# Attention and MoE block on one core: a head pair in four stages of eight score units instead of eight stages of four, and all 32 pairs written out

## The chip, the cores and the metric

One Trainium2 core (core 0) runs the whole kernel; the other seven are idle. The metric is the device time of one execution in microseconds (us), median of three runs. Each engine executes its own instruction list in order and waits for others by semaphores: PE (TensorE, matmuls), ACT (ScalarE), DVE (VectorE), POOL (GpSimd) and SP (here only a queue that issues DMAs).

## The reference

The input is 4 sequences of 1024 tokens with 128 channels, in float32. Attention has 16 heads of 64 channels, the mixture of experts has 8 experts with room for 512 tokens each. Cut to what matters:

```python
h = layernorm(x)
q, k, v = (einsum('bsd,hdk->bhsk', h, w) for w in (w_q, w_k, w_v))
weights = softmax(einsum('bhqk,bhmk->bhqm', q, k) / 8, axis=-1)
z = einsum('bhqm,bhmk->bhqk', weights, v)
x = x + h + concat_heads(z) @ w_o
h2 = layernorm(x)
probs = softmax(h2 @ Wr); expert = argmax(probs); rank = tokens of that expert before this one
y[token] = prob * (relu(h2[token] @ W1[expert]) @ W2[expert])   if rank < 512
x = x + h2 + y
```

## The kernel before, in words

**Pairs.** Two heads of one sequence are handled together, a *pair*; there are 32 pairs, 8 for each sequence, and they take most of the time. A pair works on score tiles of 128 keys by 512 queries. For each half `h` of the 1024 queries there are 8 key tiles `kt` and 2 heads `p`, so 16 *units* for a half and 32 for a pair. A unit is two matmuls on PE (`scores`, L957 and L958: high parts, then corrections and the maximum) into a PSUM bank `ps_s`, and one exponential on ACT (`unit`, L557) from that bank into the SBUF tile `ring`. POOL adds up the exponentials of each key tile for the softmax sums (`add_up`, L425), and PE multiplies them by the values into `ps_z` (`values`, L969).

**Maxima.** Before a half can start, the maximum of each query's scores must be known. PE computes plain scores for 128 queries and all keys of both heads (`max_scores`, L935, a *visit*, four matmuls into the two double banks `ps_m`), DVE reduces them (`reduce_max`, L762, twice per visit), PE turns the result (`turn_max`, L947), ACT copies it (`copy_max`, L542, tile `mxt`) and SP places it with two small DMAs. There are 8 visits per pair, made for the halves that come next.

**The next pair's operands.** Meanwhile the next pair's queries and keys are projected (`project_qk`, L914 to L916, in four uses of three matmuls), ACT casts each to its high part (`cast_qk`, L523), DVE subtracts to get the low part (`low_qk`, L757) and SP places the parts with six DMAs. `project_v` (L923) and `copy_v` (L537) make the values, `project_out` (L987) and `add_wo` (L780) the output product.

**After the values.** `softmax_sums` (L979) adds up over keys with ones on PE, DVE takes reciprocals in four quarters (`recip`, L768) and scales (`scale_z`, L775).

**The order** is written by hand. A pair has 8 *quads*: in each, PE does 4 units, with one or two projections between the second and the third, then one visit and the values of two key tiles. `ps_s` has two banks, so a unit waits for the exponential of the unit two before it. Pairs 0 and 1 and pairs 24 to 31 are written out, pairs 2 to 23 run in a loop of two pairs on every engine (`LOOP_FROM`, `UNROLL_FROM`). Pairs 0 and 1 also hold the layer norms and turns of the later sequences, and the DMAs that clear the slots in HBM (`clear_slots`, issued by ACT, all four after pair 1). In the last 8 pairs the first three sequences are routed (`routed`, roles a, b, c): moments, norm, logits, ranks, and `scatter`, eight indirect DMAs on POOL (L404), all eight in a row. The tokens' high and low parts (`h_high`, `h_low`) are made anew for every pair on ACT and POOL (L531, L411) from a copy `hTs` that a DMA brings.

**Then** the last sequence is routed, and the experts run one after the other.

## Time and profile before

| | us |
|---|---|
| median of 3 runs (lowest to highest) | 1688.39 (1686.33 to 1690.32) |
| the profiled execution, its time | 1693.12 |
| its span, first to last instruction | 1691.4 |
| PE busy | 1557.2 (92% of the span) |
| POOL busy | 1249.9 (74%) |
| DVE busy | 1071.8 (63%) |
| ACT busy | 790.6 (47%) |

The profiled execution is 4.7 us above the median, and its own time is 1.7 us above its span. Busy time of PE is modelled: the rows of two matmuls that follow each other overlap, so their starts tell more than their durations.

### The profile page before, as it was taken

How to read it: one execution, taken by the hardware profiler on the slowest of the kernel's cores; microseconds unless marked ns; L12 is line 12 of the kernel's file. 1: busy time of each engine (PE TensorE's matmuls, PEld its weight loads, DVE VectorE, ACT ScalarE, POOL GpSimd, SP SyncE). 2: the span in 40 equal slices, each digit the busy share in tenths (PEclk: the TensorE clock that was granted, in tenths of full speed). 3: DMA queues.
4: the chain of work that ended last, by engine and by line, in shares of the span. 5: the costliest groups of instructions: out<-in, count | busy, mean ns of one | idle time of the engine just before them, and what ended most of it. 6: DMA issues, size and time to landing. Idle time of an engine off the chain costs nothing.

```text
span 1691.4 us, 24966 instructions
## 1 busy us (share of the span) xinstructions
PE 1557.2 (92%) x7396; PEld 851.1 (50%) x7396; DVE 1071.8 (63%) x1316; ACT 790.6 (47%) x1543; POOL 1249.9 (74%) x713
## 2 busy tenths in 40 slices
PE   2898999999999999999999999999998989989286
PEld 1354555555555555555555555555454545544165
DVE  4565666666666767666667676666675676753332
ACT  1454555455545554545454545454554545534221
POOL 2586887777788888787888777778878778777225
PEclk8799999999999999999999999999998999989588
DMA  5333333333333333333333333333321343210430
GB/s 137 92 92 134 86 83 82 93 93 93 93 93 93 93 92 91 80 86 79 79 73 83 83 93 93 93 93 94 92 76 52 88 119 92 52 52 13 155 118 35
DMA packets 118578, 148.71 MB, mean 88 GB/s; under 512 B 41482, under 2 KB 62479, under 8 KB 118016
## 3 DMA queue, kind: packets, MB, share of 16 engines
q1 hardware_dynamic: 115392, 137.73, 32.1%
q0 software_dynamic: 2560, 6.14, 1.0%
q10 hardware_dynamic: 576, 4.23, 0.6%
q8 instruction: 26, 0.43, 0.1%
q14 instruction: 24, 0.20, 0.0%
HBM read 18.91 MB, written 12.65 MB: 19 GB/s over the span
## 4 chain that ended last, share of the span: by engine, by line
PE 82%; POOL 5%; DVE 5%; issue 3%; ACT 2%; DMA 1%; SPq 1%; another core or an unknown queue 0%; ACTq 0%; POOLq 0%; DVEq 0%
PE ps_z L969 26%; PE ps_s L957 16%; PE ps_s L958 13%; PE ps_m L935 10%; PE ps_x L979 3%; PE ps_x L987 3%; POOL acc L425 2%; DVE mxw L762 2%; PE ps_m L923 2%; PE ps_x L923 1%; POOL tokens_by_slot L404 1%; PE ps_x L914 1%; PE ps_x L915 1%; PE ps_x L916 1%; PE ps_z L1186 1%
## 5 line engine op out<-in xcount | busy, mean ns | idle before, releaser
L425 POOL TENSOR_TENSOR acc<-acc,ring 128x1024 f32<-128x1024 f32 x382 | 909.6, 2381 | 186.3 <-ACT ring L557 165.5
L557 ACT ACTIVATE ring<-ps_s 128x512 f32<-128x512 f32 x1024 | 555.9, 595 | 586.2 <-PE ps_s L958 508.0
L762 DVE TENSOR_REDUCE mxw<-ps_m 128x1 f32<-128x1024 f32 x512 | 602.9, 1219 | 234.8 <-PE ps_m L935 229.2
L969 PE MATMUL ps_z<-ring,V 128*64 128x512 f32 x2048 | 497.8, 607 | 0.0
L957 PE MATMUL ps_s<-queriesA,keysA 128*128 128x512 f32 x1024 | 450.1, 440 | 11.6 <-ACT ring L557 10.3
L958 PE MATMUL ps_s<-queriesB,keysB 65*128 65x512 f32 x1024 | 409.3, 400 | 0.0
L957 PEld LDWEIGHTS ps_s<-queriesA,keysA 128*128 128x128 f32 x1024 | 195.3, 191 | 230.8 <-issue 181.2
L768 DVE RECIPROCAL ps_x<-ps_x 128x128 f32<-128x128 f32 x256 | 221.9, 925 | 65.8 <-PE ps_x L979 65.8
L425 POOL TENSOR_TENSOR acc<-ring 128x1024 f32<-128x1024 f32 x64 | 151.2, 2363 | 135.3 <-ACT ring L557 135.3
L969 PEld LDWEIGHTS ps_z<-ring,V 128*64 128x64 f32 x2048 | 124.7, 136 | 241.5 <-issue 171.6
L935 PE MATMUL ps_m<-keysA,queriesA 64*128 64x512 f32 x1024 | 190.6, 450 | 26.3 <-DMA queriesB<-qk_rest 13.4
L958 PEld LDWEIGHTS ps_s<-queriesB,keysB 65*128 65x128 f32 x1024 | 196.6, 192 | 29.0 <-issue 1.0
L935 PEld LDWEIGHTS ps_m<-keysA,queriesA 64*128 64x128 f32 x1024 | 77.6, 187 | 150.3 <-issue 123.0
L757 DVE TENSOR_TENSOR qk_rest<-ps_x,qk_high 128x512 fp32r<-128x512 f32 x94 | 65.1, 692 | 133.0 <-ACT qk_high L523 132.9
L548 ACT ACTIVATE zr<-ps_z 128x512 f32<-128x512 f32 x64 | 38.2, 597 | 118.6 <-PE ps_z L969 114.4
L979 PE MATMUL ps_x<-acc,ones 128*64 128x512 f32 x256 | 70.0, 619 | 25.3 <-POOL acc L425 25.3
L780 DVE TENSOR_TENSOR x<-ps_x,x 128x512 f32 (+1 forms) x63 | 43.1, 685 | 53.8 <-PE ps_x L987 53.8
L411 POOL TENSOR_TENSOR h_low<-hTs,h_high 128x1024 fp32r<-128x1024 f32 x30 | 71.8, 2392 | 0.0
L987 PEld LDWEIGHTS ps_x<-wo,zT 128*128 128x128 f32 x504 | 63.7, 192 | 7.4 <-issue 0.5
L987 PE MATMUL ps_x<-wo,zT 128*128 128x128 f32 x504 | 66.4, 275 | 0.0
L460 POOL DMA_INDIRECT out<-ye,ring x32 | 31.1, 973 | 47.3 <-DVE ye L862 39.3
L523 ACT ACTIVATE qk_high<-ps_x 128x512 fp32r<-128x512 f32 x94 | 56.1, 597 | 11.3 <-PE ps_x L911 4.2
(143 smaller groups left out, 1015.7 us busy)
## 6 DMA issues: line engine op xcount, KB each, us to landing
queriesA<-qk_high SPq DMA_DIRECT2D x256, 128.0 KB, 2.4
keysA<-qk_high SPq DMA_DIRECT2D x128, 128.0 KB, 2.3
keysB<-qk_high SPq DMA_DIRECT2D x128, 128.0 KB, 2.3
keysA<-qk_rest SPq DMA_DIRECT2D x128, 128.0 KB, 2.3
queriesB<-qk_rest SPq DMA_DIRECT2D x128, 128.0 KB, 2.3
hTs<-hT SPq DMA_DIRECT2D x30, 512.0 KB, 3.3
tokens_by_slot<-rows ACTq DMA_DIRECT2D x4, 1032.0 KB, 8.7
ring<-tokens_by_slot SPq DMA_DIRECT2D x8, 516.0 KB, 7.4
```

Of the source, the lines that this page charges most:

```text
L411: pool.tensor_tensor(h_low[:, :], hTs[par][:, :], h_high[:, :].bitcast(F32), ALU.subtract).then_inc(low_split, 1)
L425: pool.tensor_tensor(acc[h][:, :], before, P_both(kt), ALU.add).then_inc(summed, 1)
L557: act.activation(P_tile(kt, p), ps_s[u % 2][:, :], ACT.Exp, scale=SCALE).then_inc(exp_done, 1)
L757: dve.tensor_tensor(qk_rest[s][:, :], qk_bank(j, use), qk_high[s][:, :].bitcast(F32), ALU.subtract).then_inc(qk_low, 1)
L762: dve.tensor_reduce(mxw[h][:, p * HT + qt:p * HT + qt + 1], ps_m[p][:, :], AX_X, ALU.max).then_inc(maxed, 1)
L768: dve.reciprocal(ps_x[:, c], ps_x[:, c]).then_inc(recip_done, 1)
L935: mm = pe.matmul(ps_m[p][:, kh * HALF:(kh + 1) * HALF], queriesA[par][p][r, at:at + P], keysA[par][p][r, kh * HALF:(kh + 1) * HALF], start ...
L957: pe.matmul(ps_s[p][:, :], keysA[par][p][:, k], queriesA[par][p][:, c], start=True, stop=False)
L958: pe.matmul(ps_s[p][:, :], keysB[par][p][:, k], queriesB[par][p][:, c], start=False, stop=True).then_inc(scores_ready, 1)
L969: mm = pe.matmul(ps_z[p * DK:(p + 1) * DK, :], V[par][:, kt * P + p * DK:kt * P + (p + 1) * DK], P_tile(kt, p), start=(kt == 0), stop=(kt ...
L979: mm = pe.matmul(ps_x[p * DK:(p + 1) * DK, :], ones[:, :], part, start=(i == 0), stop=(i == len(parts) - 1))
L987: mm = pe.matmul(bank[:, i * P:(i + 1) * P], zT[h][:, i * P:(i + 1) * P], wo[par][:, :], start=True, stop=True)
```

## The change

A pair now has 4 *octs* instead of 8 quads. In an oct PE does three units, `project_qk`, two units, then `project_v` or `project_out` (and, in every second oct, `turn_max`), three units, a visit, the values of four key tiles, in octs 0 and 2 the softmax sums, and a second visit. The counts of matmuls stay. What else changes:

- `ps_s` gets a third bank. The bank `ps_x` is gone: projections, turns and products now borrow halves of `ps_m` (`lent_qk`, `lent_turn`, `lent_out`, `lent_max`) between visits, and the softmax sums use `ps_s[2]`. So a projection waits until DVE has reduced the visit before it, and a visit waits until ACT and DVE have read what was lent.
- The sums are first copied by ACT to an SBUF tile `sums` (`copy_sums_out`, new), and `recip` and `scale_z` read that tile instead of PSUM.
- For the last of the four uses ACT writes the key's high part itself (`key_direct`), and its DMA is dropped.
- The tokens' high and low parts are made once for each sequence (at pairs 0, 6, 14 and 22) instead of once for each pair; `hTs` and its DMA are gone. `w_high` and `w_low` have two buffers.
- The slots are cleared from a small tile `blank`, one DMA at the end of each oct of pair 1. `rows` has two buffers, routing is spread over roles a to e, and a sequence's eight scatters go one at a time between the additions, six in one pair and two in the next.
- The moments of sequences 2 and 3 are taken on DVE before pair 0, and their roots on POOL.
- `LOOPED` is empty: every engine has all 32 pairs written out.

The diff, cut to its core:

```diff
-        ps_s = [ctx.enter_context(nc.psum_tensor(f"ps_s{i}", [P, HALF], F32)) for i in range(2)]
+        ps_s = [ctx.enter_context(nc.psum_tensor(f"ps_s{i}", [P, HALF], F32)) for i in range(3)]
...
+        lent_qk, lent_turn = ps_m[1][:, 0:HALF], ps_m[1][:, HALF:S]
+        lent_out, lent_max = ps_m[0][:, 0:HALF], ps_m[0][:, HALF:S]
...
+        LOOPED = []
...
+            def copy_sums_out(j, h):
+                act.wait_ge(sums_done, 2 * j + h + 1)
+                act.wait_ge(z_ready, 2 * j + h)
+                act.activation(sums[:, :], ps_s[2][:, :], ACT.Copy).then_inc(sums_copied, 1)
...
+                    for k in range(3):
+                        unit(j, oct, k)
+                    if oct < 2 and not last:
+                        cast_qk(j + 1, nxt, 2 + oct)
+                    if oct >= 2 and not known(j, LAST - 1, LAST):
+                        cast_qk(j + 2, par, oct - 2)
+                    unit(j, oct, 3)
+                    if oct in (0, 2) and not last:
+                        copy_v(j + 1, nxt, oct // 2, lent_out)
+                    unit(j, oct, 4)
...
+                if not (known(j, 0) and oct == 0 and k < 3):
+                    if k == 0:
+                        pe.wait_ge(exp_done, 2 * UNITS * j + 8 * oct)
+                    if k >= 3:
+                        pe.wait_ge(exp_done, 2 * UNITS * j + 8 * oct + k - 2)
...
-                dve.tensor_tensor(zT[h][:, :], ps_x[:, :], zr[h][:, :], ALU.mult).then_inc(z_ready, 1)
+                by = ps_s[2] if known(j, LAST) and h == 1 else sums
+                dve.tensor_tensor(zT[h][:, :], by[:, :], zr[h][:, :], ALU.mult).then_inc(z_ready, 1)
...
+                        if routed(j, "d") is not None and kt in (3, 5, 7):
+                            scatter(routed(j, "d"), [3 * h + kt // 2 - 1])
+                        if routed(j, "e") is not None and h == 0 and kt in (3, 5):
+                            scatter(routed(j, "e"), [6 + kt // 2 - 1])
...
+                    if visits:
+                        visit(v, 0)
+                    values(j, par, oct)
+                    if oct == 0 and not first:
+                        softmax_sums(j - 1, 1)
+                    if oct == 2:
+                        softmax_sums(j, 0)
+                    if visits:
+                        visit(v + 1, 1)
```

How PE's list changes in the middle of a pair. Before, after two units of a quad come the rest of that quad: a projection (L914 to L916), two units (L957, L958), a visit (L935) and the values of two key tiles (L969):

```order
L914 MATMUL ps_x<-h_high,w_low 128x512
L915 MATMUL ps_x<-h_low,w_high 128x512
L916 MATMUL ps_x<-h_high,w_high 128x512
L957 MATMUL ps_s<-queriesA,keysA 128x512
L958 MATMUL ps_s<-queriesB,keysB 128x512
L957 MATMUL ps_s<-queriesA,keysA 128x512
L958 MATMUL ps_s<-queriesB,keysB 128x512
L935 MATMUL ps_m<-keysA,queriesA 128x512 x4
L969 MATMUL ps_z<-ring,V 64x512 x4
```

Now, at the end of oct 2 of pair 0, after five units: three units (L1004, L1005), a visit (L970), the values of four key tiles (L1018), the sums (L1028) and the second visit:

```order
L1004 MATMUL ps_s<-queriesA,keysA 128x512
L1005 MATMUL ps_s<-queriesB,keysB 128x512
L1004 MATMUL ps_s<-queriesA,keysA 128x512
L1005 MATMUL ps_s<-queriesB,keysB 128x512
L1004 MATMUL ps_s<-queriesA,keysA 128x512
L1005 MATMUL ps_s<-queriesB,keysB 128x512
L970 MATMUL ps_m<-keysA,queriesA 128x512 x4
L1018 MATMUL ps_z<-ring,V 64x512 x8
L1028 MATMUL ps_s<-acc,ones 64x512 x2
L970 MATMUL ps_m<-keysA,queriesA 128x512 x4
```

Units now stand eight together where four stood, and the values eight where four did.

On ACT the copy of the values' projection (`V`) stood between two pairs of exponentials of a quad, in a written-out pair of before:

```order
L557 ACTIVATE ring<-ps_s 128x512 x2
L537 ACTIVATE V<-ps_x 128x512
L557 ACTIVATE ring<-ps_s 128x512 x2
L533 ACTIVATE w_high<-wst 128x256
```

Now it stands ahead of the fifth exponential of an oct, here in an even oct of pair 2:

```order
L569 ACTIVATE zr<-ps_z 128x512
L583 ACTIVATE ring<-ps_s 128x512 x3
L542 ACTIVATE qk_high<-ps_m 128x512
L583 ACTIVATE ring<-ps_s 128x512
L558 ACTIVATE V<-ps_m 128x512
L583 ACTIVATE ring<-ps_s 128x512 x4
```

The third unit after the copy is the eighth of the oct, which on PE waits for the fifth exponential.

On DVE, quads 1 to 3 of a written-out pair of before (reciprocals L768 from PSUM, low part L757, scaling L775, maxima L762, output added L780):

```order
L768 RECIPROCAL ps_x<-ps_x 128x128 x2
L757 TENSOR_TENSOR qk_rest<-ps_m,qk_high 128x512
L768 RECIPROCAL ps_x<-ps_x 128x128 x2
L775 TENSOR_TENSOR zT<-ps_x,zr 128x512
L762 TENSOR_REDUCE mxw<-ps_m 128x1 x2
L757 TENSOR_TENSOR qk_rest<-ps_x,qk_high 128x512
L762 TENSOR_REDUCE mxw<-ps_m 128x1 x2
L780 TENSOR_TENSOR x<-ps_x,x 128x512
```

Now, from the scaling of an even oct to the second visit of the odd oct that follows (the four reductions in a row are the first visit of one oct's end, and the second visit's, reduced in the next oct):

```order
L800 TENSOR_TENSOR zT<-sums,zr 128x512
L778 TENSOR_TENSOR qk_rest<-ps_m,qk_high 128x512
L783 TENSOR_REDUCE mxw<-ps_m 128x1 x4
L792 RECIPROCAL sums<-sums 128x128
L778 TENSOR_TENSOR qk_rest<-ps_m,qk_high 128x512
L792 RECIPROCAL sums<-sums 128x128
L805 TENSOR_TENSOR x<-ps_m,x 128x512
L783 TENSOR_REDUCE mxw<-ps_m 128x1 x2
L792 RECIPROCAL sums<-sums 128x128 x2
```

Two reciprocals, the low part and the output's addition now stand between the reductions of the last visit and those of the next one, and the scaling has both inputs in SBUF.

## Rows read from the trace of the kernel before

**Rows 1.** Busy time by stretch: PE, PEld, DVE, ACT, POOL; clock, DMA share, GB/s

```profile
600.00:700.00 100.00, 100.00 (x478) 53.80 (x475) 68.08 (x71) 50.03 (x99) 82.17 (x38) 1.00 0.31 79
```

**Rows 2.** Timeline of ACT: copies of turned maxima, one per half pair; start, duration

```profile
74.93 0.25 ACT L542 ACTIVATE mxt<-ps_m 8x128 fp32r<-8x128 f32 x1
...
150.15 0.25 ACT L542 ACTIVATE mxt<-ps_m 8x128 fp32r<-8x128 f32 x1
...
180.14 0.25 ACT L542 ACTIVATE mxt<-ps_m 8x128 fp32r<-8x128 f32 x1
...
609.33 0.25 ACT L542 ACTIVATE mxt<-ps_m 8x128 fp32r<-8x128 f32 x1
...
631.47 0.25 ACT L542 ACTIVATE mxt<-ps_m 8x128 fp32r<-8x128 f32 x1
...
654.46 0.25 ACT L542 ACTIVATE mxt<-ps_m 8x128 fp32r<-8x128 f32 x1
...
1150.92 0.25 ACT L542 ACTIVATE mxt<-ps_m 8x128 fp32r<-8x128 f32 x1
...
1173.22 0.25 ACT L542 ACTIVATE mxt<-ps_m 8x128 fp32r<-8x128 f32 x1
...
1540.05 0.25 ACT L542 ACTIVATE mxt<-ps_m 8x128 fp32r<-8x128 f32 x1
```

**Rows 3.** Timeline of PE in the loop, pieces of three quads

```profile
604.72 0.40 PE L958 MATMUL ps_s<-queriesB,keysB 65*128 65x512 f32 x1
605.05 0.73 PE L935 MATMUL ps_m<-keysA,queriesA 64*128 64x512 f32 x4
605.71 1.94 PE L969 MATMUL ps_z<-ring,V 128*64 128x512 f32 x8
607.58 0.50 PE L957 MATMUL ps_s<-queriesA,keysA 128*128 128x512 f32 x1
607.92 0.39 PE L958 MATMUL ps_s<-queriesB,keysB 65*128 65x512 f32 x1
608.15 0.39 PE L957 MATMUL ps_s<-queriesA,keysA 128*128 128x512 f32 x1
...
616.40 1.94 PE L969 MATMUL ps_z<-ring,V 128*64 128x512 f32 x8
618.16 1.03 PE L979 MATMUL ps_x<-acc,ones 128*64 128x512 f32 x4
```

**Rows 4.** Timeline of PE and of ACT around a `project_v` of a written-out pair

```profile
1490.15 1.05 PE L923 MATMUL ps_x<-wst,hTs 128*128 128x128 f32 x8
...
1491.24 0.60 ACT L537 ACTIVATE V<-ps_x 128x512 f32<-128x512 f32 x1 [0.20 <-issue]
1491.77 1.09 ACT L557 ACTIVATE ring<-ps_s 128x512 f32<-128x512 f32 x2
```

**Rows 5.** Timeline of DVE in the loop

```profile
605.82 2.35 DVE L762 TENSOR_REDUCE mxw<-ps_m 128x1 f32<-128x1024 f32 x2 [0.69 <-PE ps_m L935]
...
619.24 1.78 DVE L768 RECIPROCAL ps_x<-ps_x 128x128 f32<-128x128 f32 x2 [0.38 <-PE ps_x L979]
621.71 0.69 DVE L757 TENSOR_TENSOR qk_rest<-ps_m,qk_high 128x512 fp32r<-128x512 f32 x1 [0.69 <-ACT qk_high L523]
```

**Rows 6.** Timeline around a DVE instruction with both inputs in SBUF

```profile
1269.98 2.37 POOL L425 TENSOR_TENSOR acc<-acc,ring 128x1024 f32<-128x1024 f32 x1
...
1271.34 1.10 DVE L741 TENSOR_TENSOR logits<-one_hot,logits 128x64 f32<-128x64 f32 x1
```

**Rows 7.** Timeline of POOL and PE at a scatter: one of eight, and PE afterwards

```profile
1276.20 0.98 POOL L404 DMA_INDIRECT tokens_by_slot<-rows,scatter_at  x1 [0.30 <-issue]
...
1289.83 1.98 PE L979 MATMUL ps_x<-acc,ones 128*64 128x512 f32 x4 [7.82 <-POOL acc L425]
```

**Rows 8.** Timeline of ACT after the four clearing DMAs

```profile
160.42 1.08 ACT L557 ACTIVATE ring<-ps_s 128x512 f32<-128x512 f32 x2 [8.38 <-issue]
```

**Rows 9.** Groups by line, all of the run: xcount, busy us, mean ns, idle before

```profile
L665 DVE BATCH_NORM_STATS2 moment_parts<-x 128x6 f32<-128x128 f32 x64 | 13.8, 277 | 3.5 <-DMA x<-in_L_attn_x 3.3
```

More of the change, by code:

```diff
@@ L559, in pair @@
-            def pair(j, par, first=False, last=False, early=None, route=False, split=True, next_first=True):
+                act.wait_ge(scores_ready, 2 * UNITS * j + 8 * oct + k + 1)
+                act.activation(P_tile(kt, p), ps_s[k % 3][:, :], ACT.Exp, scale=SCALE).then_inc(exp_done, 1)
+            def pair(j, par, b):
                 nxt = 1 - par
-                a, turns = (routed(j, "a"), routed(j, "b")) if route else (None, None)
-                for quad in range(QUADS):
-                    h, u = quad // 4, 4 * (quad % 4)
-                    if not first and quad == 1:
+                last = known(j, LAST)
+                for oct in range(OCTS):
+                    if oct == 0 and not known(j, 0):
@@ L829, in _ @@
+                    if routed(j, "c") is not None and oct == 3:
+                        find_slots(routed(j, "c"), 1)
             for use in range(4):
                 low_qk(0, use)
-            for v in range(5):
+            for v in range(4):
                 for p in (1, 0):
                     reduce_max(v, v // 4, v % 4, p)
-            low_qk(1, 0)
-            pair(0, 0, first=True, early=0)
-            pair(1, 1, early=1)
-            with dve.Fori(0, LOOPS) as i:
-                for par in range(2):
-                    pair(2 * i + LOOP_FROM + par, par)
@@ L1079, in pair @@
[L1079 to L1092 removed]
+                    if c is not None and oct < 2:
+                        turn_h2(c, oct)
@@ new lines, in pair @@
+                    if c is not None and oct == 2:
+                        make_logits(c)
+                    if c is not None and oct == 3:
+                        count_ranks(c)
+                    if oct == 1:
+                        turn_max(j, 1, lent_max)
+                    if not last and oct == 3:
+                        turn_max(j + 1, 0, lent_max)
+                    for k in range(5, 8):
+                        scores(j, par, oct, k)
+                    v = 8 * j + 6 + 2 * oct
```

731 lines of the change are left out of this document (351 added, 380 removed).

## The prediction

> **What bounds the kernel now.** I read three views: the busy time by stretch, ACT's timeline for the rhythm of the pairs, and PE's timeline for what a pair consists of. In the loop PE is busy 100.00 of 100 us, DVE 68, POOL 82, ACT 50, at full clock [rows 1]: PE bounds it, and there is nothing to win by shortening a wait. The copies of the maxima mark half pairs: 609.33 to 631.47 is 22.14, 631.47 to 654.46 is 22.99, a pair is 45.13 [rows 2]. At both ends it is slower. From 74.93 to 150.15 lie three halves of pairs 0 and 1, 75.2 where the loop takes 68.1 (22.99 twice and 22.14), and the next half takes 29.99, 7.85 too much [rows 2]; there ACT had stood for 8.38 us in front of its exponentials with its own DMA issues [rows 8]. From 1150.92 to 1540.05, the last 7.5 pairs, lie 389.1 us where the loop's rate gives 338.5: 50.6 too much [rows 2].
>
> **A pair on PE, from its starts.** Two matmuls of 512 columns follow each other in 0.235 us (607.92 to 608.15) [rows 3]. The first after a visit or after values costs 0.105 more (607.58 to 607.92 is 0.34), and a visit that follows a unit starts 0.33 after its last matmul, 0.095 more than the step [rows 3]. Values of two key tiles take 1.87, but 1.76 when the sums follow them (616.40 to 618.16), so leaving them costs 0.11 [rows 3]. In a pair the octs keep every matmul and join 8 groups of units into 4 and 8 groups of values into 4. Saved: 4 entries at 0.095, 4 first matmuls at 0.105, 4 exits at 0.11: 1.24 us. Were nothing else to change a pair would take 45.13 - 1.24 = 43.9.
>
> **New waits within a pair.** *The eighth unit.* It needs the bank of the fifth, so the fifth exponential must be over. In octs 0 and 2 ACT puts the copy of V ahead of that exponential. In before's written-out pairs the copy starts 1.09 after PE began the projection (1490.15 to 1491.24), the exponential 0.53 later (1491.77), and it lasts 0.60 (two take 1.09, stepped by 0.49) [rows 4]: over at 2.22. PE spends 0.81 on the projection (1.05 less the overlap of one step), 0.08 on the change to units and 0.94 on two units, and is there at 1.83. The wait is 0.4, and 0.1 for weights that are then not loaded ahead, taken as the 0.105 above: 0.5, twice a pair. What is queued behind the unit is the visit and all values. *The visit of odd octs.* It needs DVE's addition of the output. DVE begins 0.77 after the previous visit (605.05 to 605.82 [rows 3, 5]), which itself starts 0.66 ahead of the oct: 0.1 into it. Two reductions step 2.3, a reciprocal 0.87, and the low part waits for ACT, which does three exponentials, the key's copy and the cast by about 3.5; low part 0.6 (0.69 long), second reciprocal 0.87, addition 0.7 [rows 4, 5]: 5.75. PE is there at 5.5 (0.105, eight units 3.76, `project_qk` 0.7, output 0.9). The wait is 0.3 in oct 1; in oct 3 there is no key copy, the chain is 0.5 shorter and nothing waits. Together 1.3, and a pair takes 43.9 + 1.3 = 45.2, which is before's 45.13. I count the 22 looped pairs as unchanged. Without cover each of these waits would be larger: if ACT were not idle when the copy comes, the same order would cost one more exponential each.
>
> **Other edits in the pair.** ACT's two copies of the sums cost it 0.6 each and stand where it idles behind the values (16 matmuls at 0.22, 3.5 us); SP issues 31 DMAs per pair instead of 33 (no `hTs`, no fourth key), none of them on the path. POOL loses one subtraction of 128x1024 per pair, 2.4 us by the row of an addition of that size [rows 6], in an engine with 18% to spare [rows 1]: nothing. It comes back once a sequence, three times in the middle of the run: POOL ends the half's seventh addition about 0.9 into oct 2, subtracts until 3.3, and `project_qk` wants the result at 1.5: 1.8 each, **+5** in all. That the loop is written out changes nothing by the trace: the first half of pair 24 is written out and takes 22.30, a looped one 22.14 [rows 2]. The bounds are 0 and 0.16 per half, 7 us over the looped pairs; I take 0, since that half also follows the change of the loop.
>
> **The start.** The clearing DMAs are now one per oct behind the exponentials, where ACT idles about 3.5 us: -7.85 [rows 2, 8]. Of the 7.1 in pairs 0 and 1, I keep 3 for eight token turns and their copies: -4. Sixteen moments at 0.277 and their aggregates, over 4.4 us [rows 9], now stand on DVE in front of pair 0's first projection, while the first visit starts earlier (it no longer waits for the low parts): these I set against each other, with +1. Sum **-11**, bounds -15 and -3.
>
> **The routing pairs.** PE waits 7.82 for POOL's additions behind eight scatters [rows 7]; with the slower clock and the lost exponentials, and the norm that waits for the same scatters, a scatter group costs the half about 10.8 (eight at 1.28 are 10.2). Three make 32 of the 50.6. With single scatters between additions POOL is late by 1.3 at a time and catches up; the sums leave it 9 us. So 18 remain. They grow: a sequence's logits, ranks and slots now fall into two octs, where DVE has a reduction due at the oct's start and the next projection waits for it. The slot search is some 2.5 us behind the last reciprocal, of which about 2.3 reach PE; I add 7 for three sequences. The stretch is 338.5 + 25: **-26**, bounds -33 and -8. The last octs have one more product behind them: **+1**.
>
> **Sum.** 0 + 5 - 11 - 26 + 1 = -31. From the profiled execution's own 1693.1 that gives 1662; it stood 4.7 above the median of its runs, so against 1688.4 I predict 1657 us.
>
> **A rule to weigh.** Before, `scale_z` read one input from PSUM; now both are in SBUF. A DVE instruction of only 64 columns with both inputs in SBUF took 1.10 us, more than 512 columns with one in PSUM (0.69), and ended at 1272.44, just behind the POOL addition, which ended at 1272.35 [rows 5, 6]. So such an instruction waits for the running addition, at most 2.4. The Trainium skill, "SBUF — State Buffer", section "SBUF: two separate sides", says that the port pair which VectorE and GpSimd share is an exclusive lock and that the loser blocks for the whole instruction. By that rule, the trace agrees, and the scaling waits whenever an addition runs. I walked where it falls: 2.4 into an even oct, when POOL has ended the old half's additions (0.9) and not begun the new one's, which wait for the fourth exponential (3.5). So I count nothing.
>
> **Rivals.**
> A (chance 0.66), the forecast: pairs as before, gains at both ends, own range 1640 to 1672.
> B (0.12): the two waits do not come, because ACT or DVE is a little earlier than my steps; the margins are only 0.3 to 0.5. Pairs take 43.9, 31 times 1.2 less: 1657 - 37 = 1620. Against it: the steps are the rows' own.
> C (0.10), slower: the reciprocals, now in SBUF too, wait for POOL's additions as the instruction of rows 6 did. Place: DVE in odd octs, in front of the output's addition. Two reciprocals wait up to 1.9 each, so some 3.8 per odd oct reach PE, 7.6 a pair: 1657 + 235, about 1890. It decides from 0.5 us per odd oct on (31 us over 62 odd octs), 0.25 per reciprocal. For it: both engines read SBUF. Against it: it has one input, and reductions with one input kept 2.35 beside additions [rows 5], though from PSUM.
> D (0.08): the scaling does slip onto additions, or the routing octs hold PE twice as long; low part and visit follow up to 0.3 late in each of 60 even octs: 1657 + 20, 1677, half of it near no change.
> E (0.04), slower: further waits of 0.3 or more in each oct that my walk has not found: 1657 + 37, 1694.
>
> **Numbers.** A measurement of this kernel tells a change from none at about 0.2%, 3.4 us. Faster: A, B and half of D, 0.82. Same: half of D, 0.04. Slower: C and E, 0.14. The range must leave out at most 0.2: C lies outside, and part of B; E's near side and D are in it, so 1626 to 1684.
>
> **What would show it.** In the trace after: spacing of the maxima's copies 45 us in pairs 2 to 22; PE's eighth unit of even octs released by ACT, some 0.4; the visit of oct 1 released by DVE; no 8 us gap of PE or ACT anywhere between 60 us and pair 31; scaling 0.69 long. Wrong would be: reciprocals longer than 0.93 beside POOL's additions (C), a spacing of 44 (B), or units waiting in every oct (E).

## The result and the profile after

The changed kernel took 1658.5 us (median of 4 runs, 1658.3 to 1663.5) where the kernel before took 1688.5 (1686.3 to 1690.3): a ratio of 0.983, 95% interval 0.981 to 0.985. The forecast was 1657 with a range of 1626 to 1684. Its mechanism for the steady pairs held; several of its other terms did not, and they cancelled. The kernel before moves by some 5 us from one session and chip to another (its medians are 1688.5 to 1693.6), so below each experiment is given by its ratio to before in the same session and, more sharply, by the spacing of its maxima copies: that repeats within 0.1 us per half pair in kernels with the same code there, except in the first six halves, in the routing halves (up to 0.3 either way) and where PE's clock falls. A *half* below is the time from one copy to the next.

Busy time by stretch in the changed kernel, for the same 100 us as [rows 1]: PE, PEld, DVE, ACT, POOL, clock, DMA share, GB/s.

```profile
600.00:700.00 100.00, 98.44 (x478) 55.19 (x476) 69.50 (x74) 52.52 (x103) 75.02 (x34) 1.00 0.31 72
```

PE still bounds, but 1.56 us in 100 are idle now. POOL fell from 82 to 75; over five whole pairs it is 80.4 and 75.1, the 2.4 us a pair of the subtraction that is now made once a sequence.

Timeline of ACT, the copies of the turned maxima, beside those of [rows 2]:

```profile
48.63 0.27 ACT L563 ACTIVATE mxt<-ps_s 8x128 fp32r<-8x128 f32 x1 [11.39 <-PE ps_s L989]
...
144.90 0.27 ACT L563 ACTIVATE mxt<-ps_m 8x128 fp32r<-8x128 f32 x1 [0.28 <-PE ps_m L989]
172.56 0.25 ACT L563 ACTIVATE mxt<-ps_m 8x128 fp32r<-8x128 f32 x1
...
352.89 0.25 ACT L563 ACTIVATE mxt<-ps_m 8x128 fp32r<-8x128 f32 x1
379.01 0.27 ACT L563 ACTIVATE mxt<-ps_m 8x128 fp32r<-8x128 f32 x1 [0.28 <-PE ps_m L989]
...
581.98 0.25 ACT L563 ACTIVATE mxt<-ps_m 8x128 fp32r<-8x128 f32 x1
...
627.06 0.25 ACT L563 ACTIVATE mxt<-ps_m 8x128 fp32r<-8x128 f32 x1
...
1150.95 0.27 ACT L563 ACTIVATE mxt<-ps_m 8x128 fp32r<-8x128 f32 x1 [0.28 <-PE ps_m L989]
...
1242.76 0.27 ACT L563 ACTIVATE mxt<-ps_m 8x128 fp32r<-8x128 f32 x1 [0.52 <-PE ps_m L989]
1273.09 0.25 ACT L563 ACTIVATE mxt<-ps_m 8x128 fp32r<-8x128 f32 x1
...
1510.97 0.27 ACT L563 ACTIVATE mxt<-ps_m 8x128 fp32r<-8x128 f32 x1 [0.41 <-PE ps_m L989]
```

A pair is 45.08 (581.98 to 627.06), before 45.13. Three sorts of half stick out against 22.5 (the time that "longer" and "lose" refer to below): 27.66 at the clearing transfers (144.90 to 172.56), 26.12 at a token split (352.89 to 379.01; the other two are 25.89 and 24.56), and 30.33 in a routing pair (1242.76 to 1273.09; the next sequence has 30.51, the third 25.92). With the copies numbered from 0, as in before, the change divides like this:

| stretch | before | after | forecast | measured |
|---|---|---|---|---|
| to copy 6 (203.13 before, 195.05 after) | | | -11 | -8.1 |
| three token splits, halves less 22.5 | | | +5 | +8.9 |
| the other looped pairs | 45.13 | 45.08 | 0 | -0.8 |
| copies 48 to 63, last 7.5 pairs | 389.1 | 360.0 | -26 | -29.1 |
| behind copy 63, to the end | 153.1 | 147.7 | +1 | -5.3 |
| sum | | | -31 | -34.4 |

The sum is that of the profiled executions, 1693.1 and 1658.7. The medians differ by 30.0 only: the profiled execution of before stood 4.7 above the median of its runs, that of the changed kernel 0.2. So the table compares a long execution with an ordinary one, and 4.5 of its 34.4 us are not due to the change. Which row holds them is not shown; the last one is the likely place (see *The end* below).

Timeline of PE at the end of an even oct, and three visits (of oct 0, then of octs 3 and 1):

```profile
615.19 0.40 PE L1004 MATMUL ps_s<-queriesA,keysA 128*128 128x512 f32 x1
615.42 0.40 PE L1005 MATMUL ps_s<-queriesB,keysB 65*128 65x512 f32 x1
616.07 0.50 PE L1004 MATMUL ps_s<-queriesA,keysA 128*128 128x512 f32 x1 [0.24 <-ACT ring L583]
616.40 0.40 PE L1005 MATMUL ps_s<-queriesB,keysB 65*128 65x512 f32 x1
616.73 0.73 PE L970 MATMUL ps_m<-keysA,queriesA 64*128 64x512 f32 x4
...
605.77 0.73 PE L970 MATMUL ps_m<-keysA,queriesA 64*128 64x512 f32 x4
...
628.51 0.73 PE L970 MATMUL ps_m<-keysA,queriesA 64*128 64x512 f32 x4 [0.30 <-issue]
```

The eighth unit starts 0.65 behind the matmul ahead of it, where the step is 0.235: 0.41 late, released by ACT's exponential, and the matmul behind it comes after 0.33 instead of 0.235. The visit of oct 3 (605.77) waits for nothing, that of oct 1 (628.51) does. The view names no releaser for it ("issue"); the second experiment finds it. These are the forecast's two waits, at 0.5 and 0.3.

### The profile page after: what moved, and what is told of

Same layout as the page of the kernel before. It is cut to its first block, busy times and chain, and to the rows that moved or that the text cites. A ratio compares the mean times of both kernels' runs of the same rounds, so it can differ in the third digit from the quotient of the medians.

```text
span 1656.9 us, 21749 instructions
## 1 busy us (share of the span) xinstructions
PE 1524.6 (92%) x7396; PEld 870.7 (53%) x7396; DVE 1072.0 (65%) x1316; ACT 811.3 (49%) x1586; POOL 1189.6 (72%) x687
## 4 chain that ended last, share of the span: by engine, by line
PE 85%; DVE 4%; POOL 3%; ACT 2%; issue 2%; DMA 2%; SPq 1%; POOLq 0%; DVEq 0%; ACTq 0%
PE ps_z L1018 26%; PE ps_s L1004 15%; PE ps_s L1005 13%; PE ps_m L970 10%; PE ps_m L958 3%; PE ps_s L1028 3%; PE ps_m L1036 3%; ACT ring L583 2%; PE ps_m L949 2%; PE ps_m L950 2%; PE ps_m L951 2%; DVE mxw L783 1%; POOL acc L444 1%; PE ps_m L1211 1%; PE ps_z L1211 1%
## 5 line engine op out<-in xcount | busy, mean ns | idle before, releaser
L1018 PE MATMUL ps_z<-ring,V 128*64 128x512 f32 x2048 | 471.2, 602 | 0.0
L1004 PE MATMUL ps_s<-queriesA,keysA 128*128 128x512 f32 x1024 | 441.5, 431 | 16.7 <-ACT ring L583 13.8
L1005 PE MATMUL ps_s<-queriesB,keysB 65*128 65x512 f32 x1024 | 409.8, 400 | 0.0
L1018 PEld LDWEIGHTS ps_z<-ring,V 128*64 128x64 f32 x2048 | 136.6, 137 | 268.8 <-issue 240.4
L1004 PEld LDWEIGHTS ps_s<-queriesA,keysA 128*128 128x128 f32 x1024 | 196.3, 192 | 126.6 <-issue 48.0
L792 DVE RECIPROCAL sums<-sums 128x128 f32<-128x128 f32 x252 | 228.9, 930 | 8.7 <-ACT sums L574 8.7
L970 PE MATMUL ps_m<-keysA,queriesA 64*128 64x512 f32 x1024 | 190.9, 450 | 26.9 <-DVE mxw L783 9.8
L1005 PEld LDWEIGHTS ps_s<-queriesB,keysB 65*128 65x128 f32 x1024 | 197.0, 192 | 32.2 <-issue 0.8
L970 PEld LDWEIGHTS ps_m<-keysA,queriesA 64*128 64x128 f32 x1024 | 78.5, 188 | 179.3 <-issue 153.6
L574 ACT ACTIVATE sums<-ps_s 128x512 f32<-128x512 f32 x63 | 37.7, 598 | 266.2 <-PE ps_s L1028 266.2
L778 DVE TENSOR_TENSOR qk_rest<-ps_m,qk_high 128x512 fp32r<-128x512 f32 x126 | 85.8, 682 | 46.8 <-ACT qk_high L542 29.8
L542 ACT ACTIVATE qk_high<-ps_m 128x512 fp32r<-128x512 f32 x126 | 75.4, 599 | 43.0 <-PE ps_m L951 23.0
L1036 PEld LDWEIGHTS ps_m<-wo,zT 128*128 128x128 f32 x512 | 67.8, 194 | 11.8 <-issue 6.0
L1036 PE MATMUL ps_m<-wo,zT 128*128 128x128 f32 x512 | 68.7, 277 | 4.3 <-DVE zT L800 4.3
L958 PEld LDWEIGHTS ps_m<-wst,hT 128*128 128x128 f32 x496 | 69.1, 202 | 6.2 <-DVE mxw L783 0.2
L958 PE MATMUL ps_m<-wst,hT 128*128 128x128 f32 x496 | 69.1, 285 | 0.0
L1028 PE MATMUL ps_s<-acc,ones 128*64 128x512 f32 x256 | 66.7, 593 | 0.0
```

The lines of the kernel that those rows point to most:

```text
L778: dve.tensor_tensor(qk_rest[s][:, :], qk_bank(j, use), qk_high[s][:, :].bitcast(F32), ALU.subtract).then_inc(qk_low, 1)
L792: dve.reciprocal(sums[:, c], sums[:, c]).then_inc(recip_done, 1)
L958: mm = pe.matmul(bank[:, i * P:(i + 1) * P], hT[:, t:t + P], wst[par][:, 4 * DK:6 * DK], start=True, stop=True)
L970: mm = pe.matmul(ps_m[p][:, kh * HALF:(kh + 1) * HALF], queriesA[par][p][r, at:at + P], keysA[par][p][r, kh * HALF:(kh + 1) * HALF], start ...
L1004: pe.matmul(ps_s[k % 3][:, :], keysA[par][p][:, t], queriesA[par][p][:, c], start=True, stop=False)
L1005: pe.matmul(ps_s[k % 3][:, :], keysB[par][p][:, t], queriesB[par][p][:, c], start=False, stop=True).then_inc(scores_ready, 1)
```

## The experiments

**The eighth unit.** Exponential 5 goes ahead of the copy of V on ACT.

```diff
-                    if oct in (0, 2) and not last:
-                        copy_v(j + 1, nxt, oct // 2, lent_out)
                     unit(j, oct, 4)
+                    if oct in (0, 2) and not last:
+                        copy_v(j + 1, nxt, oct // 2, lent_out)
```

> The changed kernel with one pair of statements on ACT exchanged: in octs 0 and 2 the fifth exponential stands ahead of the copy of V. The trace of the changed kernel has PE's eighth unit of these octs 0.41 us late (a step of 0.65 where others are 0.235) and 0.1 more for the matmul behind it. Theory 1 (the forecast's step): that wait is ACT's order alone, so 0.5 goes twice a pair and 62 times in all: pairs of 44.1 instead of 45.1, 31 us off 1658, 1627 us. Theory 2: the copy of V, now 0.5 later, makes the visit behind the eighth unit wait instead, or the weight load is late anyway: pairs stay within 0.2 of 45.1, 1652 to 1660 us.

Measured: ratio 0.9647 (0.9627 to 0.9667). A pair is 44.07 (two copies of its ACT timeline, one pair apart):

```profile
595.06 0.27 ACT L563 ACTIVATE mxt<-ps_m 8x128 fp32r<-8x128 f32 x1 [0.28 <-PE ps_m L989]
...
639.13 0.27 ACT L563 ACTIVATE mxt<-ps_m 8x128 fp32r<-8x128 f32 x1 [0.28 <-PE ps_m L989]
```

PE at the same place, where every step is now 0.235 and the visit 0.33:

```profile
606.00 0.40 PE L1005 MATMUL ps_s<-queriesB,keysB 65*128 65x512 f32 x1
606.23 0.40 PE L1004 MATMUL ps_s<-queriesA,keysA 128*128 128x512 f32 x1
606.47 0.40 PE L1005 MATMUL ps_s<-queriesB,keysB 65*128 65x512 f32 x1
606.80 0.50 PE L970 MATMUL ps_m<-keysA,queriesA 64*128 64x512 f32 x2
```

Theory 1: 1.01 a pair less, and the eighth unit waits no more, so the wait was ACT's order alone.

**The visit of oct 1.** The addition of the output goes ahead of the second reciprocal, in both odd octs.

```diff
-                        recip(j - 1, 1, 1)
                         add_out(j - 1, 0, before, lent_out)
+                        recip(j - 1, 1, 1)
```

> The changed kernel with DVE's second reciprocal of odd octs behind the addition of the output instead of ahead of it. The visit of oct 1 starts 0.36 us late in the trace of the changed kernel, which the forecast put down to this addition. Theory 1: the addition then ends 0.9 earlier, the wait goes, 0.3 to 0.4 a pair, 31 pairs: 10 to 12 us off 1658, about 1647 us. Theory 2: the visit starts late because of something else (the placed operands, the copy of the maxima): no change, 1656 to 1660 us. Theory 3: the reciprocal now runs into the visit's reductions and they make the next projection wait: slower by up to 0.5 a pair, 1674 us.

Measured: 0.9771 (0.9755 to 0.9787). From copy 21 to 29 the distance to the changed kernel grows from -1.6 to -3.0, 0.35 a pair, and PE's list of waits from 300 to 350 us no longer has the visit. Theory 1.

**The token split.**

```diff
-                        if known(j, *range(HP - 2, PAIRS - HP, HP)) and (h, kt) == (1, 1):
+                        if known(j, *range(HP - 2, PAIRS - HP, HP)) and (h, kt) == (0, 7):
                             split_low_tokens(b + 1)
```

> The changed kernel with POOL's low part of the tokens, once a sequence, one addition earlier: ahead of the seventh of half 0 instead of the first of half 1. In the trace of the changed kernel the three half pairs with it are 3.6, 3.3 and 2.0 us longer than others, the projection's wait for it is 1.8 in each. Theory 1: the whole 8.9 comes from this wait (what is beyond 5.4 is a lower granted clock behind it), so about 9 us go: 1650 us. Theory 2: only the waits go: 5 us, 1653 us. Theory 3: the addition pushed back makes the sums wait: no gain, 1656 to 1660 us.

Measured: 0.9764 (0.9748 to 0.9781). The three halves lose 3.6, 3.4 and 2.1 us, 9.0 in all; the first is now 354.66 to 377.19, 22.53. Theory 1. PE's wait for the split, and the stretches around the first and the third split in the changed kernel:

```profile
PE ps_m L949 <- POOL h_low L432: 1.8, 1, 1.8
```

```profile
352.90:379.00 26.10, 23.73 (x107) 13.34 (x106) 16.44 (x17) 12.57 (x25) 18.83 (x8) 0.93 0.11 26
...
1081.30:1105.90 24.60, 22.26 (x108) 12.16 (x108) 16.49 (x17) 12.51 (x26) 18.88 (x8) 1.00 0.12 27
```

The wait is 1.8 in all three. Where the granted clock stays at 1.00 (2.4 GHz) that is all the half loses, 2.0; where the pause is followed by a fall to the lower level, the stretch's mean is 0.93 and the half loses 1.3 to 1.6 more. Which of the three falls changes from run to run of the same code: in the kernel with loops (below) the same halves are 24.56, 27.13 and 24.57.

**The slot search.** Its second part goes from the end of oct 3 into oct 0 of the next pair, behind the low part.

```diff
-                    if routed(j, "c") is not None and oct == 3:
-                        find_slots(routed(j, "c"), 1)
+                    if routed(j, "d") is not None and oct == 0:
+                        find_slots(routed(j, "d"), 1)
```

> The changed kernel with the second part of DVE's slot search in oct 0 of the next pair, behind the low part, instead of at the end of oct 3. In the trace of the changed kernel two instructions of 8 columns in it take 2.17 and 2.19 us in two sequences and 0.17 in the third; both long ones end where a POOL addition ends. PE then waits 5.4, 5.4 and 2.0 for a reduction. Theory 1 (DVE instructions with all operands in SBUF wait for POOL's running addition, and the chain is in front of a reduction that is due): in the new place DVE idles about 4 us and POOL is between two halves, so the chain is short or hidden: the three halves lose 7.8, 7.9 and 3.4 us, 19 us off 1658, 1640 us. Theory 2: the long times are of the instructions themselves (first use, chained waits) and only the place matters: the two instructions are 2.2 long again, and 15 to 19 us go all the same. Theory 3: the scatters, whose index is now later, hold POOL up: no gain.

In the changed kernel, timeline of DVE and of POOL where the half of 30.33 loses its time, and the matmul of PE that waits:

```profile
1248.84 0.70 DVE L762 TENSOR_TENSOR logits<-one_hot,logits 128x64 f32<-128x64 f32 x1
1249.58 0.22 DVE L763 TENSOR_REDUCE routing_columns<-logits 128x8 f32<-128x64 f32 x1
1249.84 2.17 DVE L765 TENSOR_SCALAR routing_columns<-routing_columns 128x8 f32<-128x8 f32 x1
1251.92 0.16 DVE L766 TENSOR_SCALAR routing_columns<-routing_columns 128x8 f32<-128x8 f32 x1
1252.11 0.17 DVE L767 TENSOR_TENSOR routing_columns<-routing_columns 128x8 f32<-128x8 f32 x1
1252.31 2.19 DVE L768 TENSOR_TENSOR scatter_at<-routing_columns 128x8 int32<-128x8 f32 x1
...
1249.61 4.87 POOL L444 TENSOR_TENSOR acc<-acc,ring 128x1024 f32<-128x1024 f32 x2
1252.12 2.36 POOL L444 TENSOR_TENSOR acc<-acc,ring 128x1024 f32<-128x1024 f32 x1
...
1256.02 0.79 PE L949 MATMUL ps_m<-h_high,w_low 128*128 128x512 f32 x1 [5.36 <-DVE mxw L783]
```

The first POOL line holds two additions, which start at 1249.61 and 1252.12 (the second line shows the later one by itself); the later one ends at 1254.48, the earlier one just ahead of it, near 1252.0. The DVE instructions of 8 columns that started inside them end at 1252.01 and 1254.50; the two that start around 1252, between them, take 0.16 and 0.17. Measured with the edit: 0.9759 (0.9736 to 0.9781); the three halves lose 5.6, 5.8 and 2.8, 14.1 together, where the theories said 19. The place was not as idle as I expected of theory 1: the two instructions take 1.99 and 2.22 again in the first two sequences, since POOL's additions run late there, and PE waits 2.1 for the reduction behind them. Theory 2's forecast of the durations came true, but not its reason, which the run with two inputs (below) tells apart: they end with POOL's additions.

**Scatters in one block.**

```diff
-                        if routed(j, "d") is not None and kt in (3, 5, 7):
-                            scatter(routed(j, "d"), [3 * h + kt // 2 - 1])
-                        if routed(j, "e") is not None and h == 0 and kt in (3, 5):
-                            scatter(routed(j, "e"), [6 + kt // 2 - 1])
+                        if routed(j, "d") is not None and (h, kt) == (0, 3):
+                            scatter(routed(j, "d"), range(QT))
```

> The changed kernel with the eight scatters of a sequence in one block, ahead of the third addition of half 0 of the pair behind the slot search, instead of one at a time between additions of two pairs. The two buffers for the rows stay. Theory 1 (the forecast's 10.8 a group): eight scatters hold POOL for 10.2 us, the sums wait for POOL as before the change: three halves longer by 5 to 10 us, 15 to 30 us more, 1680 us. Theory 2: POOL has enough reserve now (75% busy) and what the change won came from the two buffers: at most 5 us more, 1658 to 1664 us.

Measured: 0.9818 (0.9801 to 0.9834); copies 48 to 63 are 358.9 apart, 1.1 less than with spread scatters. Theory 2's time: spreading them is worth nothing here. Its reason, the two buffers, was not tried by itself. The block takes 10.2 us of POOL; the last addition of that half then ended at 1286.9 and PE's sums started at 1288.0, so 1.1 us of slack were left.

**The same question in the kernel before**, its block one addition later than the deadline that it missed.

```diff
-                        if c is not None and (h, kt) == (0, 6):
+                        if c is not None and (h, kt) == (1, 1):
                             scatter(c)
```

> The kernel BEFORE with one edit: its block of eight scatters stands ahead of POOL's first addition of half 1 instead of the sixth of half 0. The block is as long, the single buffer for the rows stays. Theory 1 (what the change won in the routing pairs is the slack between the scatters and the sums that wait for POOL, since with the changed kernel a block of eight cost nothing): PE's three waits of 7.8, 7.8 and 7.4 us for POOL's additions go or shrink to 2, with the lower clock behind them: 15 to 28 us less than before's 1688.5, about 1667 us. Theory 2: the same 10 us come back as a wait for the low parts of tokens and weights, which stand two additions behind the block, or for the norm: within 5 us of 1688. Theory 3: the two buffers are what counts: no change.

Measured: 0.9964 (0.9951 to 0.9976). PE's waits from 1150 us to the end of the pairs, first in before, then with the block moved (us in total, times, longest):

```profile
PE ps_x L979 <- POOL acc L425: 23.0, 3, 7.8
PE ps_s L957 <- ACT ring L557: 3.7, 6, 2.5
```

```profile
PE ps_s L957 <- ACT ring L557: 11.7, 9, 3.5
PE ps_x L914 <- POOL w_low L413: 6.5, 2, 4.7
...
PE ps_x L979 <- POOL acc L425: 0.7, 1, 0.7
```

Theory 2: the wait for the sums went, and some 14 of its 22 us came back as waits for the weights' low part and for ACT, whose norm waits 10.5 for POOL. In the first two sequences the move lost 6.3 in all; in the third, behind which no norm and no split stands, it won 9.6 and the next half lost 1.0.

**Clearing transfers in one block.**

```diff
-                    if known(j, 1):
-                        clear_slots(oct)
+                    if known(j, 1) and oct == 1:
+                        for n in range(4):
+                            clear_slots(n)
```

> The changed kernel with all four clearing transfers issued by ACT behind oct 1 of pair 1 instead of one behind each oct. Theory 1 (the forecast's 7.85): ACT stands about 8 us with the issues, PE waits for exponentials: 6 to 9 us more, 1666 us. Theory 2: four transfers of 1 MB already delay the placing of operands when spread (the half from 144.90 to 172.56 is 27.66 long, 5.1 too much), and as a block they only delay it once: within 3 us of 1658.

Measured: 0.9801 (0.9784 to 0.9817). The half up to copy 4 is 4.2 longer, the one behind it 5.1 shorter. Theory 2. The two halves together are 52.2 us, inside the 50.6 to 54.5 of the kernels that issue the four apart and have the same code there, so ACT's stand was not what had to be removed: something costs as much when the four are apart.

**Clearing transfers one a pair, and half the moments later.**

```diff
-            for b in (2, 3):
-                for g in range(2):
-                    first_moments(b, g)
+            for g in range(2):
+                first_moments(2, g)
...
+                    if first and oct == 0:
+                        for g in range(2):
+                            first_moments(3, g)
...
-                    if known(j, 1):
-                        clear_slots(oct)
+                    if known(j, 2, 3, 4, 5) and oct == 1:
+                        clear_slots(j - 2)
```

> The changed kernel with two edits at the start, seen in different half pairs. First: the moments of sequence 3 (2.7 us of DVE) stand behind the first oct's low part, their inverse root ahead of POOL's fifth addition. The first half pair is 26.59 long in the changed kernel, PE waits 3.1, 2.5 and 2.4 for DVE around it. Theory: 2.7 less by the second copy of the maxima; rival: nothing, another wait follows. Second: the four clearing transfers are issued one per pair in pairs 2 to 5 instead of one per oct in pair 1. In the changed kernel the half from 144.90 is 27.66 long, and it was not shorter in sum when the four stood in one block. Theory 1 (four transfers of 1 MB within 45 us hold up the placing of operands, wherever ACT issues them): that half is 22.5 to 23, 5 us less, and none of the later ones is longer. Theory 2: each transfer costs its own 1.3 us somewhere: no sum less. In all 1650 us by the theories, 1658 by the rivals.

Measured: 0.983 (0.9813 to 0.9846), as the unedited change. The moments: 2.5 less in the first half, 1.7 more in the second; rival's side. The transfers: without them the halves of pair 1 lose 3.0 and 5.1, and the halves with one are 4.0, 2.3, 5.5 and 3.9 longer, 15.7 in all. Both theories fail: a transfer costs more by itself, two to five us. (The 3.0 and 5.1 are against the changed kernel's own halves; against the five kernels with the same code there, the two together lose 5.7 to 9.6.) PE in the first unit of the half behind one, and PE's waits from 40 to 320 us:

```profile
221.14 0.50 PE L1008 MATMUL ps_s<-queriesA,keysA 128*128 128x512 f32 x1 [2.21 <-DMA queriesB<-mxt]
```

```profile
PE ps_s L1008 <- DMA queriesB<-mxt: 9.3, 4, 2.5
```

The clearing transfer was issued at 213.69 behind oct 1, the 4 KB of turned maxima from 214.73 on, and PE waits for them until 221.14. Their landing is not recorded; the small transfer just ahead of them, issued at 214.1, took 6.7 us to land, where its kind takes 2.4 in the median, and the 1 MB landed at 220.73. So the small ones land behind the large one. In an oct 0 or 2 no maxima are turned.

**All edits together:** those of the first four experiments and both of the start.

> The changed kernel with the edits of the earlier experiments together: fifth exponential ahead of the copy of V, addition of the output ahead of the second reciprocal, low part of the tokens one addition earlier, second part of the slot search in the next pair, and both edits of the start. Theory 1 (the waits are independent): halves of 22.06 and 21.64 on average, pairs of 43.7 (45.08 less 1.02 and 0.37), which is the forecast's 43.9 without waits; 31 + 11 + 9 + 12 + 7 = 70 us off 1658, 1588 us. Theory 2: with PE faster by 3% POOL or the chain of operands becomes late (in the first of these experiments one routing pair lost 1.7 of its gain): 1595 to 1610 us.

Measured: 0.9527 (0.9508 to 0.9545). Pairs are 43.7, as theory 1 says. By the ratio (0.9527 against 0.983) 19 us are missing to 1588. Of these some 13 are the clearing transfers, which I had put down as a gain of 5 and which cost 15.7 - 8.1 = 7.6 net by the preceding experiment; the rest lies in the start, the routing pairs and the end.

**All edits but those of the start, and the clearing transfers behind even octs.**

```diff
-                    if known(j, 1):
-                        clear_slots(oct)
+                    if known(j, 1, 2) and oct in (0, 2):
+                        clear_slots(2 * (j - 1) + oct // 2)
```

> The combined kernel without the two edits of the start; instead the clearing transfers stand behind octs 0 and 2 of pairs 1 and 2, two each. Theory 1 (a transfer of 1 MB costs where the maxima are copied in the same oct, since theirs then lands behind it; behind an even oct nothing is due): the halves of pairs 2 to 5, which took 26.0, 25.6, 25.9 and 25.7 with a transfer in the combined kernel, are 21.7 like the others, 15.8 us less over the first six pairs; the halves of pairs 1 and 2 stay within 1 us of those without transfers: ratio to before 0.9527 - 0.0093 = 0.943, about 1596 us. Theory 2 (each transfer costs 2 to 5 us wherever it stands): as the combined kernel, 0.950 to 0.955, 1605 to 1615 us.

Measured: 1598.8 us, ratio 0.9453 (0.9437 to 0.9469): the fastest kernel of the study, 3.8% below the changed one. By copy 12 it is 17.0 ahead of the kernel with all edits. The four halves in which a transfer is issued are 22.25, 22.29, 22.05 and 21.65 long, as they are without one, so a transfer behind an even oct costs nothing; theory 1. (In the kernel with all edits, whose transfers come later, the first three of these are 22.25, 22.29 and 22.05.) Two copies one pair apart (600.92 to 644.62, 43.70):

```profile
600.92 0.25 ACT L563 ACTIVATE mxt<-ps_m 8x128 fp32r<-8x128 f32 x1
...
644.62 0.25 ACT L563 ACTIVATE mxt<-ps_m 8x128 fp32r<-8x128 f32 x1
```

**Loops put back.**

```diff
-        LOOPED = []
+        LOOPED = [(2, 2), (10, 2), (18, 2)]
```

> The changed kernel with pairs 2 to 5, 10 to 13 and 18 to 21 back in loops of two pairs (two iterations each), the other 20 written out. Theory 1 (the forecast's 0 for writing the loop out): no change, 1655 to 1662 us, halves of 22.5 inside loops. Theory 2: a loop's branch costs 0.3 us or more per iteration on the engine that bounds, or a written-out pair costs 0.3 more: 2 to 4 us one way or the other. Theory 3: entering and leaving a loop costs some us each on PE: 6 to 12 us more.

Measured: 0.9826 (0.9809 to 0.9843), no change that the time can tell. The copies tell more: 1.2, 1.3 and 1.0 us over the three loops of four pairs, 0.3 a pair, each time in the half that begins with the visit of oct 1. Theory 2 in its size, but not by PE's branch, which comes once in two pairs. The visit, and what stands ahead of it on DVE and SP:

```profile
538.86 0.73 PE L970 MATMUL ps_m<-keysA,queriesA 64*128 64x512 f32 x4 [0.46 <-DMA queriesA<-qk_high]
...
537.81 0.63 DVE L805 TENSOR_TENSOR x<-ps_m,x 128x512 f32<-128x512 f32 x1
...
536.33 0.46 SPq L303 DMA_DIRECT2D queriesA<-qk_high  x1
```

The view puts the wait down to a transfer, but the last one that the visit can need, issued at 536.33, landed at 538.52, 1.37 behind the copy of the maxima (537.15), and in the written-out kernel at the same place it landed 1.37 behind. DVE's addition ended at 538.44. What differs is PE's own sequencer: its trace has four register instructions there (L976, L977, L978, L966 at 538.47, 538.57, 538.67 and 538.76), one for each of four semaphore waits of the program, and the visit starts at 538.86. Written out, PE has two wait instructions there, which its sequencer has begun before the addition is over, and the visit starts 0.10 behind the addition instead of 0.42.

**Two inputs in SBUF.** The kernel leaves out the reciprocal, so its output is another.

```diff
-                    dve.reciprocal(sums[:, c], sums[:, c]).then_inc(recip_done, 1)
+                    dve.tensor_tensor(sums[:, c], sums[:, c], sums[:, c], ALU.mult).then_inc(recip_done, 1)
```

> The changed kernel with each reciprocal of 128 columns in SBUF replaced by a product of the same columns with themselves, an instruction with two inputs in SBUF. It leaves out the reciprocal, so the output is another. Theory 1 (the forecast's rival C with the right instruction: two inputs in SBUF wait for POOL's running addition, one input doesn't): these products, 0.2 us long by themselves, take 1 us and more each, up to 2.4, and in odd octs reach PE through the addition of the output: 0.5 to 4 us per odd oct, 1690 to 1900 us. Theory 2: the products are 0.2 us long where the reciprocals took 0.93, nothing waits, and the visit of oct 1 is not late any more: 10 us less, 1648 us.

Measured: 1803.6 us, ratio 1.0668 (1.065 to 1.0686), pairs of 50.4 on average. The same line in the changed kernel and in this one, all of the run (ns min/median/max), and DVE and POOL in an odd oct of this one:

```profile
L792 DVE RECIPROCAL sums<-sums x252: 891/942/954, 95.2 to 1529.6; 128x128 f32<-128x128 f32 x126
```

```profile
L792 DVE TENSOR_TENSOR sums<-sums x252: 274/1979/3039, 96.4 to 1676.7; 128x128 f32<-128x128 f32 x126
...
620.40 2.16 DVE L792 TENSOR_TENSOR sums<-sums 128x128 f32<-128x128 f32 x1
...
623.09 1.99 DVE L792 TENSOR_TENSOR sums<-sums 128x128 f32<-128x128 f32 x1
...
620.05 4.88 POOL L444 TENSOR_TENSOR acc<-acc,ring 128x1024 f32<-128x1024 f32 x2 [2.09 <-ACT ring L583]
622.56 7.37 POOL L444 TENSOR_TENSOR acc<-acc,ring 128x1024 f32<-128x1024 f32 x3
```

The product needs 0.27 and takes 1.98 in the median: one that starts inside an addition (620.40) ends when the addition ends and the next one (622.56) begins. Theory 1. The reciprocal, one input in SBUF, never took more than 0.95 beside the same additions; the low part, one input in PSUM, kept its 0.69. The Trainium skill, "SBUF — State Buffer", section "SBUF: two separate sides", has VectorE and GpSimd share one port pair under an exclusive lock, taken by VectorE for two SBUF inputs or in a two-port mode. By that rule, the traces agree: the products wait and the reciprocals don't. `TENSOR_SCALAR` of the slot search has one input and waits as well (2.17 against 0.17), which fits the two-port mode; no run shows in which mode it ran.

## Why the prediction came out right

*The pair, "a pair takes 43.9 + 1.3 = 45.2".* Right, and in its parts. Without the two waits the pair measured 43.70 against 43.9 (the 0.2 may be the loop, see below), the eighth unit gave back 1.01 against 1.0, and the visit of oct 1 0.35 against 0.3. The change had thus won 1.4 us a pair and given 1.4 back: some 40 us in the run, the place where most of its gain went. Rival B is refuted for the changed kernel and is what the two exchanges make of it.

*The token split, "+5".* The wait was right (1.8, three times, 5.4). The step left out what follows a pause of PE: in two of three cases the granted clock fell behind it, and the term is 8.9. That it was two is of this execution: other executions of the same code had one case or another.

*"The clearing DMAs are now one per oct behind the exponentials [...] -7.85".* This step failed. ACT no longer stands for 8 us in front of its exponentials, but spread over pair 1 the transfers cost 3.0 and 5.1 us in its halves, since the copied maxima land behind 1 MB. The forecast asked what holds up the engine that issues, not what queues behind the transfer. That the start was -8.1 all the same, against -11, is due to what the forecast did not count on: copy 0 came 3.6 us earlier, and copies 1 to 4 lie 69.7 apart instead of 75.2 with three of the transfers among them; the cause of both is open. The first half, where I had put the moments with +1, is 3.9 longer. The term is not sharp: copy 6 stands at 192.6 to 197.0 in kernels with the same code up to it, so -8.1 may be anything from -6 to -11.

*The routing pairs, -26.* Measured -29.1, with the right main term (the waits of 23.0 for POOL's additions are gone) for a reason that was half right at most. "Single scatters between additions" is not it, since a block does as well. Moving the block in before shows that the slack for the sums is not all either: the norm and the low parts behind the block must have it too. Which of the changed kernel's looser deadlines (a later norm, two buffers, one subtraction less a pair) carries how much was not separated. "I add 7 for three sequences" was too little: the three halves lose 7.8, 7.9 and 3.4, 19. The step "the slot search is some 2.5 us behind the last reciprocal" took its instructions at their own length. The rule that I had weighed for `scale_z` applied to them: two of 0.17 us wait for POOL's running addition, some 4 us in front of a reduction that PE waits for. I had walked it through the steady pairs only.

*`scale_z`, "I count nothing".* Right for the steady pairs: 0.68 long at 613.06, in POOL's gap, and so in 51 of 63 cases. At the three token splits it takes 1.5, and in the last eight pairs 1.2 to 4.5. The longest, in the changed kernel, and POOL beside it:

```profile
1499.61 4.51 DVE L800 TENSOR_TENSOR zT<-sums,zr 128x512 f32<-128x512 f32 x1
...
1498.83 2.41 POOL L444 TENSOR_TENSOR acc<-acc,ring 128x1024 f32<-128x1024 f32 x1
1501.17 2.38 POOL L444 TENSOR_TENSOR acc<-ring 128x1024 f32<-128x1024 f32 x1
```

"At most 2.4" was wrong: with no gap between two additions it waited for both. This is half of rival D's mechanism. No wait of PE from 1150 to 1511 us is put down to it, so no price of it shows.

*Rival C.* False for the reciprocals (0.93 in the mean), and true to its mechanism: with two inputs in SBUF at the same place the kernel is slower than before by 6.7% and than the changed one by 8.5%. Its price was too high: 5.3 a pair measured, 7.6 forecast; the first of the two stands where DVE would wait for ACT anyway, which may be the difference.

*The written-out loop, 0, bounds 0 and +7.* Outside them, and with the other sign: in the changed kernel it is the loops that cost 0.3 a pair, some 7 us over 22 pairs. The step looked at half a pair of before in which the loop also ended. Whether before's loops cost as much is not shown, as its waits are at other places; if they do, joining the stages won 1.1 of the 1.4 a pair, and leaving the loop the other 0.3.

*The end, +1.* It measured -5.3. From copy 63 to the end of the span the changed kernel and its versions with blocks, loops or products take 146 us, its other versions, with the same code there, 149 to 151, and before 151. As far as these runs show, that goes by the session in which a profile was taken and not by the edit: those four versions were run together. From copy 63 on, PE falls behind by some 0.4 us at a time in the experts' matmuls of the long ones, with the same code. So most of the 5.3 is no effect of the change, and may well be the 4.5 by which the two profiled executions differ from their medians; what decides between the two was not found.

So the small error of the sum is a balance, and in part luck. On the profiled executions, -31 was forecast and -34.4 measured. Longer than forecast were the clearing (8), the slot search (12) and the splits (4), 24 us; shorter the end (6), the rest of the routing pairs (15) and of the start (5), 26 us, and the pairs by 1. The 1657 then took off another 4.7 for before's profile, which the changed kernel's did not need; so 1662 for the profile was 3 too long, and 1657 for the median 1.5 too short.

## What to carry to other kernels

When work is merged into longer stages, the copies and additions between them stand in front of the next dependent unit; walk each engine's order once more, for one exchange of two statements here gave 1 us a pair where the change had won 1.4 and kept none. Before placing a large transfer, ask whose small transfer comes right behind it, and put it where none is due. Price a DVE instruction with two SBUF inputs by POOL's longest instruction, not by its own length, wherever a reduction waits behind it, and do not count on one such wait: it can be two when POOL leaves no gap. Try one block before spreading: what matters is the slack to each dependent.

## What was not expected of the hardware

- A DVE `TENSOR_SCALAR` of 8 columns with one SBUF input took 2.17 us inside a POOL addition and 0.16 in the gap between two; `RECIPROCAL` (at most 0.95) and `TENSOR_REDUCE` (0.22) from SBUF never did. A held instruction can miss its turn: one of 0.68 us took 4.51, over two additions.
- A pause of PE of 1.8 us was followed by a lower granted clock in two places and not in the third, and in other places in another run; the fall cost 1.3 to 1.6 us, nearly as much as the pause.
- A 1 MB transfer (7.5 us to landing) issued 1 us ahead of 4 KB held PE for up to 2.5 us and cost a half pair 2.3 to 5.5.
- In a loop, PE's sequencer spent four register instructions, 0.1 us apart, on waits in front of a matmul, after the event that it waited for; that cost 0.3 us a pair. The loop's branch cost nothing that shows, and the transfers came no later.
